# The last eight terms of a head attention's products added on TensorE instead of GpSimd, with a new order of items in a decoder layer

## The chip, the core and the metric
The kernel runs on one core of a Trainium2 chip. The metric is the device time of one execution in microseconds (us). Inside a core TensorE (PE) multiplies matrices into PSUM, VectorE (DVE), ScalarE (ACT) and GpSimd (POOL) work element by element, and SyncE (SP) issues the DMAs. The engines run side by side, each in its own written order, and wait for each other by semaphores.

## The reference
One decoder layer over 2048 tokens of 256 features, fp32, in three parts, each on the layer norm of x and added to x:
```
q, k, v = x@Wq.T, x@Wk.T, x@Wv.T, as 16 heads of 16; q, k rotated (rope); q's heads permuted
scores = einsum('bshd,bstd->bsht', q, k) / 4            # within one token, head against head
attn   = einsum('bsht,bstd->bshd', softmax(scores), v);  x += attn @ Wo.T
q = fake_quant(x@Wxq + b); k, v = fake_quant(cond@Wkv + b)   # 2048 keys, 16 heads of 16
p = fake_quant(softmax(q@k.T));  x += (p@v) @ Wp + b
scores = sigmoid(x@gate.T); two of 8 experts per token; x += shared + routed silu MLP
```
The first part matters here: per token a 16x16 table of scores, each a sum of 16 products over d, and a 16x16 table of outputs, each a sum of 16 products over t.

## The kernel before, in words
The 2048 tokens are 16 tiles of 128 tokens, a token to a partition. A stage ahead of the loop (steps u = 0 to 9) makes the quantised keys and values of all 2048 conditions. Then `body(t)` runs over the tiles, and in it h runs over the 16 heads of the cross attention of tile t. Around this spine lie the other parts, each for another tile: a = t+2 gets layer norm 0, q, k, v, rope and the scores of its head attention; n = t+1 gets the rest of its head attention, layer norm 1 and its quantised queries; m = t-1 gets the end of its cross attention, layer norm 2, gate and shared expert; o = t-2 gets the experts and the store.

The spine of one head: TensorE makes the scores of 128 tokens against 2048 keys in two halves (`scores(h, 0, t)`, `scores(h, 1, t)`, L1459) into two PSUM buffers that take turns. VectorE scales each half into SBUF and takes its minimum (`keep_scores`, L1135), then makes the bias (L1145). ScalarE takes the exponent (`exp_head`, L824). SP issues a DMA transpose of the result (`turn`, L423). TensorE multiplies four transposed heads by the values in 64 products (`times_values(0)`, `(G)`, `(2G)`, `(3G)`, L1489). There are four buffers each of score and prob and six of transposed prob, so turn n waits for the products of head n-6.

Each engine's order is written out by hand: in its `body(t)` a list of items, each with the head h at which it stands, is gone through for every h. On VectorE, TensorE and ScalarE the items stand around the spine's own items. The places that matter, before:
- SP, `body` L435: `turn_routed(t-1)` at h=13, `load_x(t+3)` (L375, waits for one_done) at h=15 ahead of `turn(15, t)`, `store(t-2)` (L403, waits for `add_out` of VectorE) at h=2 behind `turn(2, t)`.
- GpSimd, head attention: `multiply` (L522) makes 4 of the 16 rows at a time into one of four product buffers, 1024 products per partition. `fold_one` (L529) adds terms 8 to 15 to 0 to 7. `fold_8`, `fold_4`, `fold_2` (to L567) add on down to one, over two buffers at a time, into hs (scores) or ho (outputs). `shift_scores` (L478) subtracts the maximum that VectorE found, `norm_ho` (L483) multiplies by the inverse sum.
- VectorE, `body` L1219: `loaded(a)` and bn_stats of x_in (L1075) at h=0 behind `keep_scores(0)`; bn_stats of the projected head attention (L1075, waits for L1424) at h=8; `cross_norm(m)` h=5; `choose(m)` h=10; `largest_score(a)` and `quantise_queries(n)` h=13; `add_out(o)` h=3.
- TensorE, `body` L1563: `ho_turn(n)` and `ho_project(n)` (L1416, L1424) at h=8, the projection right behind `times_values(0, t)`; `times_values(3G, m)` h=5; `times_values(G, t)` h=12; `times_values(2G, t)` h=15.
- ScalarE, `body` L887: `ln_apply(0, a)` behind exp 0, `ln_keep(0, a)` ahead of exp 1, `keep_qkv(0, a)` ahead of exp 2 (L770).

TensorE runs about one head ahead of VectorE, bound by the two buffers:
```
def wait_slot(u):
    if u >= 2:
        kind, n, i = USES[u - 2]
        if kind == "score":
            pe.wait_ge(score_kept, 2 * n + i + 1)
```
The bank `ps_pv` holds the output of times_values in its first 256 columns; `bank` 5, 6 and 7 serve the other products by turns.

## Time and profile before
| | us |
|---|---|
| median of 3 runs | 1065.17 |
| lowest, highest | 1061.33, 1065.57 |
| the profiled execution, its own time | 1068.14 |
| its span in the profile | 1065.7 |
| mean granted clock of TensorE, of 2.4 GHz | 0.838 |

The profiled execution is 3.0 us over the median. In the rows PE is TensorE, PEld its weight loads, DVE VectorE, ACT ScalarE, POOL GpSimd, SPq the DMA queue of SP. L12 is line 12 of the kernel; several products share line 1317, a helper. Loading, keys and values take the time up to 92.5 us, where the first score is read; tile 1 begins at 159 us, tile 14 at 921 us.

### The profile page before, as it was taken

To read this page: it belongs to the slowest core of one execution; us is meant where nothing else is said; L and a number is where in the kernel's file an instruction comes from. 1 tells how busy PE (TensorE), PEld (TensorE's weight loads), DVE (VectorE), ACT (ScalarE), POOL (GpSimd) and SP (SyncE) were. 2 spreads that over 40 slices of the span, in tenths; PEclk is the share of its full clock that TensorE was granted. 3 is DMA by queue.
4 is the path that set the end of the run, shared out by engine and by line. 5 is a ranking of instruction groups with operands and counts; after the bars stand their busy time and mean duration, and the time that the engine had idled before them with its cause. 6 is when DMAs were issued, how large, how long until landed. Compare 5 with 4: busy or idle time off the path is not lost. (4 is left out here: it accounts for less than half of the span.)

```text
span 1065.7 us, 21210 instructions
## 1 busy us (share of the span) xinstructions
PE 722.0 (68%) x7072; PEld 388.6 (36%) x7072; DVE 906.5 (85%) x1841; ACT 737.3 (69%) x989; POOL 746.9 (70%) x728
## 2 busy tenths in 40 slices
PE   6966647666675867675776758576667767675674
PEld 4543323333342524343332425243333324242333
DVE  3887769989888899989898989899888989999851
ACT  2644656868677776868686877778686868878742
POOL 6688987787786778787886868787878868730000
PEclk9975777888896978889897989888878979798965
DMA  6012767979698896979797999979697979999981
GB/s 225 1 40 70 133 119 140 186 115 192 128 176 147 150 173 127 187 114 198 120 194 144 160 168 146 190 121 188 129 179 115 192 150 169 172 167 182 162 161 25
DMA packets 574019, 156.01 MB, mean 146 GB/s; under 512 B 567252, under 2 KB 571863, under 8 KB 573527
## 3 DMA queue, kind: packets, MB, share of 16 engines
q1 hardware_dynamic: 573910, 154.67, 81.5%
q8 instruction: 56, 0.92, 0.3%
q14 instruction: 53, 0.43, 0.1%
HBM read 9.93 MB, written 2.10 MB: 11 GB/s over the span
## 5 line engine op out<-in xcount | busy, mean ns | idle before, releaser
L1135 DVE TENSOR_SCALAR_CACHE_REDUCE score<-ps_score,q_neg 128x1024 f32<-128x1024 f32 x512 | 636.2, 1277 | 17.2 <-PE ps_score L1459 15.9
L824 ACT ACTIVATE prob<-score,exp_bias 128x2048 uint16<-128x2048 f32 x256 | 512.1, 2001 | 61.4 <-DVE exp_bias L1145 58.5
L1459 PE MATMUL ps_score<-keys,queries 128*128 128x512 bf16 x1024 | 368.1, 450 | 255.4 <-DVE score L1135 248.7
L1459 PEld LDWEIGHTS ps_score<-keys,queries 128*128 128x128 bf16 x1024 | 72.2, 103 | 445.7 <-DVE score L1135 415.9
L527 POOL TENSOR_TENSOR product<-hs_exp,v_tok 128x1024 f32<-128x1024 f32 x64 | 149.4, 2347 | 31.0 <-ACT hs_exp L789 30.8
L534 POOL TENSOR_TENSOR product<-product 128x512 f32<-128x512 f32 x128 | 159.5, 1262 | 0.0
L527 POOL TENSOR_TENSOR product<-qk_rot 128x1024 f32<-128x1024 f32 x64 | 150.2, 2349 | 0.3 <-POOL qk_rot L520 0.2
L1489 PE MATMUL ps_pv<-prob_t,values 128*32 128x128 f16 x4096 | 74.2, 229 | 25.1 <-DMA prob_t<-prob 24.8
L545 POOL TENSOR_TENSOR product<-product 128x512 f32<-128x512 f32 x64 | 80.8, 1271 | 5.9 <-POOL product L534 5.9
L1489 PEld LDWEIGHTS ps_pv<-prob_t,values 128*32 128x32 f16 x4096 | 63.2, 101 | 55.2 <-issue 55.2
L466 POOL TENSOR_SCALAR var_eps<-mean_var 128x1 f32<-128x1 f32 x48 | 12.6, 262 | 90.2 <-DVE mean_var L1080 89.2
L884 ACT ACTIVATE early<-ps 128x512 f32<-128x512 f32 x32 | 19.1, 597 | 67.8 <-DVE early L1188 61.6
L768 ACT COPY normed_t<-ps 128x256 f32<-128x256 f32 x48 | 18.0, 376 | 65.1 <-PE ps L1322 65.1
L481 POOL TENSOR_TENSOR hs<-hs,hs_max 128x256 f32<-128x256 f32 x16 | 10.0, 622 | 69.3 <-DVE hs_max L1084 69.3
L1317 PE MATMUL ps<-routed_both,w 128*128 128x128 bf16 x512 | 45.0, 249 | 18.6 <-DMA routed_both<-routed_both 16.9
L877 ACT ACTIVATE routed_both<-normed,routed_gate 128x256 bf16<-128x256 f32 x128 | 55.4, 493 | 1.2 <-DVE routed_gate L1180 1.2
L1145 DVE TENSOR_SCALAR exp_bias<-low 128x1 f32<-128x1 f32 x256 | 52.0, 203 | 2.8
L1317 PEld LDWEIGHTS ps<-routed_both,w 128*128 128x128 bf16 x512 | 39.4, 113 | 35.9 <-DMA routed_both<-routed_both 21.7
L824 ACT ACTIVATION_READ_ACCUMULATOR prob<-score,exp_bias 128x1 f32 x256 | 48.9, 191 | 0.0
L502 POOL COPY sum_wide<-sum_inv 128x128 f32<-128x128 f32 x32 | 8.5, 296 | 52.0 <-DVE sum_inv L1152 52.0
L552 POOL TENSOR_TENSOR product<-product 128x256 f32<-128x256 f32 x64 | 39.7, 629 | 5.9 <-POOL product L545 5.9
L1135 DVE DVE_READ_ACCUMULATOR score<-ps_score,q_neg 128x1 f32 x512 | 42.3, 83 | 0.0
(124 smaller groups left out, 1112.2 us busy)
## 6 DMA issues: line engine op xcount, KB each, us to landing
prob_t<-prob SPq DMA_TRANSPOSE x256, 4.5
prob_t<-in_w SPq DMA_DIRECT2D x3, 1024.0 KB, 4.8
x_in<-in_x SPq DMA_DIRECT2D x16, 128.0 KB, 3.0
score<-in_cond_t SPq DMA_DIRECT2D x4, 512.0 KB, 6.3
out<-x_out SPq DMA_DIRECT2D x16, 128.0 KB, 2.7
w_qkv<-in_w_qkv SPq DMA_DIRECT2D x1, 768.0 KB, 4.4
early<-in_w_kv SPq DMA_DIRECT2D x1, 512.0 KB
w_s<-in_w_s SPq DMA_DIRECT2D x3, 128.0 KB
```

The costliest lines, as they stand in the source:

```text
L527: pool.tensor_tensor(product[:, i % 4], a_, b_, ALU.mult).then_inc(multiplied, 1)
L534: pool.tensor_tensor(terms[:, :, 0:8], terms[:, :, 0:8], terms[:, :, 8:16], ALU.add).then_inc(folded_8, 1)
L545: pool.tensor_tensor(terms[:, :, 0:4], terms[:, :, 0:4], terms[:, :, 4:8], ALU.add).then_inc(folded_4, 1)
L552: pool.tensor_tensor(terms[:, :, 0:2], terms[:, :, 0:2], terms[:, :, 2:4], ALU.add).then_inc(folded_2, 1)
L824: act.activation(prob[:, s, :].bitcast(U16), score[:, s, :], ACT.Exp, bias=exp_bias[:, s:s + 1], scale=-1.0, accum_out=prob_sum[:, t.par, ...
L877: act.activation(routed_tok[:, e, :], normed[:, 2, :], ACT.Copy, scale=routed_gate[:, e:e + 1]).then_inc(routed_made, 1)
L884: act.activation(tanh[:].rearrange("p e q -> p (e q)"), bank[(5, 7)[i]][:, :], ACT.Tanh, scale=0.5).then_inc(hidden_tanhed, 1)
L1135: dve.tensor_scalar(score[:, s, HALF * i:HALF * i + HALF], ps_score[:, score_slot(t.count(H, h), i)].rearrange("p b k -> p (b k)"), q_neg[ ...
L1145: dve.tensor_scalar(exp_bias[:, s:s + 1], low[:, s, 0:1], low[:, s, 1:2], LN255, ALU.min, ALU.add).then_inc(bias_ready, 1)
L1317: mm = pe.matmul(out, lhs[c], rhs[c], start=start and c == 0, stop=stop and c == C - 1)
L1459: mm = pe.matmul(ps_score[:, score_slot(n, i), b, :], queries[:, t.par, h // 2, h % 2, :], keys[:, h // 2, k0:k0 + KEYS], start=True, stop ...
L1489: mm = pe.matmul(out[j], beside_zeros(values, i, h + j), prob_t[:, t.count(H, h + j) % KEPT, i, :], start=(i == 0 and first), stop=(i == T ...
```

## The change
The products of the head attention are folded once on GpSimd, from 16 to 8 terms, and the 8 terms are added by 8 fp32 matmuls with the identity as weights, which accumulate in PSUM (`sum_terms`, four per tile, each over two product buffers, so 128 columns with a step of 16 elements in SBUF). The sums lie in bank 7 for tiles 0 and 1 and in the free half of the bank of `ps_pv` after, and times_values waits for their readers (`wait_pv`). VectorE takes the maximum there, and now also does the shift and the division. hs_exp and ho_n come out as before.

The items of all engines have new places. SP: `store(t-2)` at h=0 ahead of `turn(0, t)`, `load_x(t+3)` at h=13 behind `turn(13, t)`. VectorE: bn_stats of x_in stays at h=0; `add_out(o)` 2, both `expert_hidden(o)` 1, `sum_scores(n)` 1, `cross_sum(m)` 2, `cross_norm(m)` 4, bn_stats(2, m) 5, `norm_ho(n)` 8 and bn_stats(1, n) 10 ahead of keep_scores, `choose(m)` 11, `largest_query(n)` 12, `quantise_queries(n)` 14 and `shift_scores(a)` 15 ahead of keep_scores, `largest_score(a)` 14 behind it. TensorE: `ln_turn(0, a)` 3, `times_values(3G, m)` 4 between the two score halves, `queries_or_keys(a)` and `xo_project(m)` 5, `sum_terms(2, n)` 6 and `(3, n)` 7, `ho_turn(n)` and then `times_values(0, t)` 8, `ho_project(n)` 9, `gate_and_shared(m)` and `times_values(G, t)` 11, `sum_terms(0, a)` 13 and `(1, a)` 14, `q_turn(n)` and `times_values(2G, t)` 15; the sums stand behind scores(h, 1). ScalarE: `ln_apply(0, a)` 2, `ln_keep(0, a)` and `keep_xo(m)` 3, `keep_qkv(a)` 4 and 6, `keep_ho(n)` 7, all ahead of that head's exp, `keep_queries(n)` 14, `head_exp(a)` 15. In tile 0 the items of n come two heads later.

The core of the diff (the re-ordered lists of VectorE, TensorE and ScalarE are the text above):
```diff
         v_tok = sb("v_tok", [P, HD, H])
-        product = sb("product", [P, 4, G, H, HD])
+        product = sb("product", [P, 4, G * H, HD])
+        k_max = sb("k_max", [P, 2 * H])
...
         def own_bank(t):
-            return bank[5 if t.idx < 2 else 7]
+            return bank[5 if t.idx < 3 else 7]
+
+        def sums_of(t):
+
+            return (bank[7] if t.idx < 2 else ps_pv)[:, D:2 * D]
...
             def body(t):
                 for h in range(H):
+                    if (t + -2).exists() and h == 0:
+                        store(t + -2)
                     if (t + -1).exists() and h == 13:
                         turn_routed(t + -1)
-                    if (t + 3).exists() and h == 15:
-                        load_x(t + 3)
                     if t.exists() and by_dma(h):
                         turn(h, t)
-                    if (t + -2).exists() and h == 2:
-                        store(t + -2)
+                    if (t + 3).exists() and h == 13:
+                        load_x(t + 3)
...
-            def shift_scores(t):
-                pool.wait_ge(hs_shift, t.count(2, 1))
-                pool.sem_inc(settled, 1)
-                pool.tensor_tensor(hs[:], hs[:], over(hs_max[:], H), ALU.subtract).then_inc(hs_shift, 1)
-            def norm_ho(t):
-                pool.wait_ge(reduced, t.count(4, 4))
...
-                pool.tensor_tensor(ho_n[:], ho[:], over(hs_inv[:], HD), ALU.mult).then_inc(ho_done, 1)
...
             def multiply(i, t, a_, b_):
-                    pool.wait_ge(reduced, due)
+                    pool.wait_ge(summed, due)
                     pool.sem_inc(settled, 1)
-                pool.tensor_tensor(product[:, i % 4], a_, b_, ALU.mult).then_inc(multiplied, 1)
-            def fold_one(i, t):
+                out = product[:, i % 4].rearrange("p (g h) d -> p g h d", g=G)
+                pool.tensor_tensor(out, a_, b_, ALU.mult).then_inc(multiplied, 1)
+
+            def fold(i, t):
+                terms = product[:, i % 4]
                 pool.wait_ge(multiplied, t.count(8, i + 1))
                 pool.sem_inc(settled, 1)
-                pool.tensor_tensor(terms[:, :, 0:8], terms[:, :, 0:8], terms[:, :, 8:16], ALU.add
...
-            def fold_8(i, t):
-                terms = both(i)
-                pool.wait_ge(folded_8, t.count(8, 2 * i + 2))
-                pool.sem_inc(settled, 1)
...
-            def fold_4(i, t):
...
-            def fold_2(i, t):
...
+                pool.tensor_tensor(terms[:, :, 0:HD // 2], terms[:, :, 0:HD // 2], terms[:, :, HD // 2:HD],
+                                   ALU.add
+                    ).then_inc(folded, 1)
...
             def body(t):
                 a, n, m = t + 2, t + 1, t + -1
                 if n.exists():
-                    value_products(2, n)
-                if m.exists():
-                    spread_sums(m)
+                    value_products(0, n)
+                    fold(4, n)
+                    value_products(1, n)
+                    fold(5, n)
                 if a.exists() and not t.starts():
                     ln_scale(0, a)
                 if n.exists():
+                    value_products(2, n)
+                    fold(6, n)
+                if m.exists():
+                    spread_sums(m)
+                if n.exists():
                     value_products(3, n)
-                    fold_one(6, n)
-                    fold_one(7, n)
-                    fold_8(3, n)
-                    fold_4(3, n)
-                    fold_2(3, n)
+                    fold(7, n)
                 if a.exists():
                     rope(a)
-                if n.exists():
-                    norm_ho(n)
-                if a.exists():
                     score_products(0, a)
+                    fold(0, a)
                 if m.exists():
                     ln_scale(2, m)
                 if a.exists():
                     score_products(1, a)
-                    fold_one(0, a)
+                    score_products(2, a)
+                    fold(1, a)
+                    score_products(3, a)
                 if n.exists():
                     ln_scale(1, n)
                 if a.exists():
-                    score_products(2, a)
-                    fold_one(1, a)
-                    score_products(3, a)
-                    fold_one(2, a)
-                    fold_one(3, a)
-                    fold_8(0, a)
-                    fold_8(1, a)
-                    fold_4(0, a)
-                    fold_4(1, a)
-                    fold_2(0, a)
-                    fold_2(1, a)
-                    shift_scores(a)
-                    value_products(0, a)
-                    value_products(1, a)
-                    fold_one(4, a)
-                    fold_one(5, a)
-                    fold_8(2, a)
-                    fold_4(2, a)
-                    fold_2(2, a)
...
             def all_scores(t):
-                score_products(0, t)
...
-                fold_2(1, t)
+                for j in range(0, G, 2):
+                    score_products(j, t)
+                    score_products(j + 1, t)
+                    fold(j, t)
+                    fold(j + 1, t)
+
+            def half_values(j, t):
+                value_products(j, t)
+                value_products(j + 1, t)
+                fold(G + j, t)
+                fold(G + j + 1, t)
...
             def largest_score(t):
-                dve.wait_ge(reduced, t.count(4, 2))
-                dve.tensor_reduce(hs_max[:], hs[:], AX.X, ALU.max).then_inc(hs_shift, 1)
+                dve.wait_ge(summed, t.count(4, 2))
+                dve.tensor_reduce(hs_max[:], heads(sums_of(t)), AX.X, ALU.max).then_inc(hs_shift, 1)
+
+            def shift_scores(t):
+                dve.wait_ge(hs_shift, t.count(2, 1))
+                if (due := t.due(1)) is not None:
+                    dve.wait_ge(hs_exped, due)
+                dve.tensor_tensor(hs[:], heads(sums_of(t)), over(hs_max[:], H), ALU.subtract).then_inc(hs_shift, 1)
+
+            def norm_ho(t):
+                dve.wait_ge(summed, t.count(4, 4))
+                dve.wait_ge(hs_summed, t.count(2, 2))
+                if (due := t.due(1)) is not None:
+                    dve.wait_ge(ho_turned, due)
+                dve.tensor_tensor(ho_n[:], heads(sums_of(t)), over(hs_inv[:], HD), ALU.mult).then_inc(ho_done, 1)
...
@@ -1287,18 +1213,20 @@
                     loaded(second)
                     ln_gather(0, x_in[:, 1, :], second)
                     ln_combine(0, second)
-                if u == 4:
                     largest_score(first)
+                    shift_scores(first)
                 if u == 5:
                     value_maxima(0)
                 if u == 6:
+                    cast_experts(0)
                     sum_scores(first)
                     invert_sums(first)
-                    cast_experts(0)
-                if u == 8:
+                    norm_ho(first)
+                if u == 7:
                     dve.wait_ge(ho_projected, 1)
                     ln_gather(1, one_bank(first)[:, 0:D], first)
                     ln_combine(1, first)
...
@@ -1306,6 +1234,8 @@
             cast_experts(1)
             keep_first_values(0)
             keep_first_values(1)
+            largest_score(second)
+            shift_scores(second)
...
             def ho_turn(t):
                 pe.wait_ge(ho_done, t.count(1, 1))
-                if t.starts():
-                    pe.wait_ge(qkv_kept, 4)
+                if t.idx < 2:
+                    pe.wait_ge(qkv_kept, t.count(2, 4))
...
@@ -1477,10 +1407,9 @@
                         pe.wait_ge(prob_turned[n % KEPT], 16 * count_dma(n + 1, n % KEPT))
                 if (made := count_pe(t.count(H, h + G))) > 0:
                     pe.wait_ge(turn_kept, made)
-                if h == 0:
-
-                    if (due := t.due(1)) is not None:
-                        pe.wait_ge(xo_kept, due)
+                wait_pv()
+                if h == 3 * G:
+                    read["xo"] = t.idx + 1
...
+            read = {"shift": 0, "ho": 0, "xo": 0}
+
+            def wait_pv():
+
+                if read["shift"] > 0:
+                    pe.wait_ge(hs_shift, 2 * read["shift"])
+                if read["ho"] > 0:
+                    pe.wait_ge(ho_done, read["ho"])
+                if read["xo"] > 0:
+                    pe.wait_ge(xo_kept, read["xo"])
+
+            def sum_terms(i, t):
+
+                pe.wait_ge(folded, t.count(8, 2 * i + 2))
+                if t.idx < 2:
+                    if i == 2:
+                        pe.wait_ge(hs_shift, t.count(2, 2))
+                    if t.idx == 1 and i == 0:
+                        pe.wait_ge(ho_done, 1)
+                else:
+                    wait_pv()
+                out = sums_of(t)[:, P * (i % 2):P * (i % 2) + P]
+                for d in range(HD // 2):
+                    mm = pe.matmul(out, ident[:], product[:, 2 * (i % 2):2 * (i % 2) + 2, :, d], start=d == 0,
+                                   stop=d == HD // 2 - 1)
+                mm.then_inc(summed, 1)
+                if t.idx > 1 and i % 2 == 1:
+                    read[("shift", "ho")[i // 2]] = t.idx + 1
...
@@ -1649,10 +1614,18 @@
                 if u == 9:
                     ln_turn(1, first)
                     xq(first)
+                if u == 4:
+                    sum_terms(1, first)
+                if u == 6:
+                    sum_terms(2, first)
+                if u == 7:
+                    sum_terms(3, first)
                 keys_and_values(u)
+                if u == 3:
+                    sum_terms(0, first)
+                if u == 4:
+                    ln_turn(0, second)
                 if u == 5:
-                    ln_turn(0, second)
-                if u == 6:
                     queries_or_keys(0, second)
                     queries_or_keys(1, second)
                     own_values(0, second)
@@ -1662,6 +1635,8 @@
             q_turn(first)
             turn_values(2)
             turn_values(3)
+            sum_terms(0, second)
+            sum_terms(1, second)
```

## Rows read from the trace of the kernel before

**Rows 1.** The page, part 1: busy time, share of the span, instructions of each engine
```profile
PE 722.0 (68%) x7072; PEld 388.6 (36%) x7072; DVE 906.5 (85%) x1841; ACT 737.3 (69%) x989; POOL 746.9 (70%) x728
```

**Rows 2.** Busy time by stretch: stretch, length, engines, TensorE clock share, DMA share, GB/s
```profile
686.10:744.40 58.30, 39.18 (x428) 21.07 (x426) 53.23 (x112) 43.98 (x60) 46.18 (x46) 0.88 0.94 160
921.10:973.00 51.90, 34.87 (x402) 17.97 (x402) 50.25 (x109) 42.54 (x57) 19.12 (x22) 0.93 0.99 175
```

**Rows 3.** Waits of VectorE, 158.9 to 921.2 us: total us, times, longest
```profile
DVE stats L1075 <- DMA x_in<-in_x: 37.4, 13, 3.8
DVE stats L1075 <- PE ps L1424: 25.7, 13, 3.8
```

**Rows 4.** Timeline of VectorE: start us, us, instruction, idle before and releaser
```profile
159.00 0.41 DVE L1088 TENSOR_REDUCE hs_sum<-hs_exp 128x16 f32<-128x256 f32 x1
...
744.36 0.41 DVE L1088 TENSOR_REDUCE hs_sum<-hs_exp 128x16 f32<-128x256 f32 x1
...
750.56 0.43 DVE L1075 BATCH_NORM_STATS2 stats<-x_in 128x6 f32<-128x256 f32 x1 [3.07 <-DMA x_in<-in_x]
...
778.72 0.43 DVE L1075 BATCH_NORM_STATS2 stats<-ps 128x6 f32<-128x256 f32 x1 [3.25 <-PE ps L1424]
...
921.13 0.41 DVE L1088 TENSOR_REDUCE hs_sum<-hs_exp 128x16 f32<-128x256 f32 x1
```

**Rows 5.** Timeline of SP's queue; the last row is 10 transposes issued without a gap
```profile
747.39 0.93 SPq L380 DMA_DIRECT2D x_in<-in_x  x1
...
755.13 1.44 SPq L423 DMA_TRANSPOSE prob_t<-prob  x1
...
766.57 1.86 SPq L423 DMA_TRANSPOSE prob_t<-prob  x1
...
769.71 1.90 SPq L423 DMA_TRANSPOSE prob_t<-prob  x1
...
994.11 27.09 SPq L423 DMA_TRANSPOSE prob_t<-prob  x10
```

**Rows 6.** Timeline of TensorE's products
```profile
663.47 0.69 PE L1317 MATMUL ps<-normed_t,w_s 128*128 128x128 f32 x4
...
770.49 0.59 PE L1459 MATMUL ps_score<-keys,queries 128*128 128x512 bf16 x2
...
774.50 1.78 PE L1489 MATMUL ps_pv<-prob_t,values 128*32 128x128 f16 x64 [1.01 <-DMA prob_t<-prob]
```

**Rows 7.** Groups by line, GpSimd: busy us, mean ns | idle before
```profile
L545 POOL TENSOR_TENSOR product<-product 128x512 f32<-128x512 f32 x64 | 80.8, 1271 | 5.9 <-POOL product L534 5.9
L552 POOL TENSOR_TENSOR product<-product 128x256 f32<-128x256 f32 x64 | 39.7, 629 | 5.9 <-POOL product L545 5.9
L567 POOL TENSOR_TENSOR ho<-product 128x128 f32<-128x128 f32 x32 | 13.0, 406 | 7.0 <-POOL product L552 7.0
L491 POOL TENSOR_TENSOR ho_n<-ho,hs_inv 128x256 f32<-128x256 f32 x16 | 10.0, 624 | 0.6 <-POOL ho L567 0.6
```

**Rows 8.** Groups by line, VectorE: an operation of 128x256 with an operand in PSUM
```profile
L1160 DVE TENSOR_TENSOR xo_t<-ps,xo_raw 128x256 f32<-128x256 f32 x16 | 6.7, 420 | 3.1 <-PE ps L1500 3.1
```

**Rows 9.** Groups by line: TensorE's fp32 products of 128 columns, ScalarE's copies from PSUM
```profile
L1317 PE MATMUL ps<-normed_t,w_s 128*128 128x128 f32 x128 | 21.5, 294 | 0.0
L768 ACT COPY normed_t<-ps 128x256 f32<-128x256 f32 x48 | 18.0, 376 | 65.1 <-PE ps L1322 65.1
L780 ACT COPY v_tok<-ps 128x256 f32<-128x256 f32 x16 | 9.6, 598 | 2.1 <-POOL product L527 0.9 <-PE ps L1405 0.6
```

**Rows 10.** Timeline of TensorE's products in the last tile's tail
```profile
1046.33 2.05 PE L1317 MATMUL ps<-normed_t,w_s 128*128 128x128 f32 x8
```

**Rows 11.** Waits of VectorE, 93 to 158.9 us
```profile
DVE hs_max L1084 <- POOL hs L567: 10.2, 2, 7.3
DVE score L1135 <- PE ps_score L1459: 9.3, 5, 3.8
```

**Rows 12.** Busy time by stretch, in the stage ahead of the loop (columns as in Rows 2)
```profile
28.00:66.00 38.00, 35.67 (x194) 21.68 (x194) 33.09 (x55) 22.83 (x34) 29.45 (x26) 1.00 0.09 29
```

367 lines of the change are left out of this document (155 added, 212 removed).

## Prediction
> **What bounds the kernel now.** I read the busy shares first: VectorE is busy 85% of the span, GpSimd 70%, ScalarE 69%, TensorE 68% [rows 1]. Then two stretches of one tile each: in a tile of 58.3 us VectorE is busy 53.2 us, GpSimd 46.2, ScalarE 44.0, TensorE 39.2, and the DMA share is 0.94 [rows 2]. So VectorE sets the pace, and what can still be won is its idle time. The list of its waits from 158.9 to 921.2 us names it [rows 3]: 37.4 us in 13 waits for x_in and 25.7 us in 13 waits for TensorE's projection of the head attention (line 1424), with 2.3 us of others 65.4 in all. From hs_sum of tile 1 at 159.00 to hs_sum of tile 14 at 921.13 13 tiles take 762.1 us, 58.6 each, and the timeline shows one wait of each sort per tile, in the one that starts at 744.4 of 3.07 and 3.25 us [rows 4]. Without them a tile would take 53.6 us.
>
> Why they are there: load_x(t+3) stands before turn(15, t) in SP's queue and comes out only after turn(14, t). It is issued at 747.39 and lands 3 us later, while bn_stats stands ready behind head 0 [rows 4, 5]. The second wait ends with the projection: TensorE stands 1.01 us for the transposed head 3 (turn 3 was issued at 769.71, 25 us into the tile, behind the store), then does 64 products in 1.78 us and right behind them the projection, in one burst with two score buffers before it [rows 4 to 6].
>
> **The change, part by part.**
>
> 1. *GpSimd loses* the folds of 8, 4 and 2 terms, the shift and the division: 80.8 + 39.7 + 13.0 for ho and 12.2 for hs in a like group + 10.0 for the division and as much for the shift = 165.7 us, 10.4 per tile [rows 7]. The fold from 16 to 8 stays. In the steady state I cost this at nothing: GpSimd has 12 us of slack per tile. It counts early on, where GpSimd is late: VectorE waits 10.2 us for hs in tile 0 [rows 11].
>
> 2. *VectorE gains* two operations of 128x256 from PSUM. The nearest row is the 128x256 tensor_tensor from PSUM, 420 ns [rows 8]: 0.84 us per tile, and nothing covers it, since VectorE is the bound. Bounds 0.7 to 1.0. For 13 tiles +10.9 us.
>
> 3. *TensorE gains* four sums of 8 fp32 identity products per tile, each a 128x128 product. By w_s, one such product is two records, so a sum is 16 records. At the full clock 4 records take 0.69 us [rows 6], of which about 0.15 is the latency of the last, as a score pair of 0.59 us shows against 0.43 for 2 x 512 columns at 2.4 GHz: some 0.13 to 0.14 each. At the low clock 8 take 2.05, or 0.26 each [rows 10]; the mean over the kernel is 21.5/128 = 0.168 [rows 9]. A sum is thus 2.1 us at 2.4 GHz, 4.1 at 1.2, 2.7 in the mean, and TensorE goes from 39.2 to about 50 us per tile, under VectorE's 54.4. What counts is where the bursts lie, because scores have two buffers only. Between scores(h,1) and scores(h+1,0) VectorE has two score operations of 1.2 us and the bias to do, 2.6 us, of which the two score products take 0.9: a burst up to 1.6 is hidden. At h=6 a sum of 2.1 to 2.7 shows 0.5 to 1.1. At h=7 the division (0.42) follows, slack 1.9: 0.2 to 0.8. At h=13 the 2.2 us of quantise_queries come next, slack 4. At h=14 they come before largest_score needs the sum, slack 3.5; at 4.1 us that one shows 0.6. I take 1.2 us per tile, nearest to the full clock rows, because a score pair ahead of h=7 takes 0.59 us already, the full clock's time [rows 6], and the idle time of TensorE behind the x_in wait goes. Bounds 0 and 5 (all sums at 4.1). For 13 tiles +15.6 us.
>
>    What no row shows is a moving operand read with a step of 16 fp32. The nearest row is on another engine: ScalarE's copy into v_tok writes 256 elements with such a step in 598 ns, the plain copy of 256 takes 376 [rows 9]. So from below it costs nothing; from above it takes 598/376 = 1.6 of the time, 3.4 us a sum at full clock. I take nothing, since the fp32 product here is paced by its two records with their own weight loads, not by elements alone, and keep the other end as a rival. The Trainium skill (SBUF — State Buffer, section Door 1) says SBUF has 16-byte lines and that each access to a new line pays, so a stride is free only to 4 fp32; by that rule this operand pays on every element and the time would be that of the first rival. The v_tok row agrees with it; on TensorE no row of this trace tells.
>
>    The sums lie in the bank of ps_pv from tile 2 on, so times_values and the sums wait for the last reader of that bank. times_values(0) at h=8 waits for ho_done, times_values(2G) at h=15 for the shift that VectorE now does ahead of head 15. Behind it in TensorE's queue are scores(9,0) and the next tile's scores. Both readers run about 0.6 and 1.0 us after VectorE frees the second buffer, TensorE needs 0.45 of that for scores: under 0.6 us, inside the slack. GpSimd's products wait for summed: the score products 0 for the sum at h=6, when it still does rope. Nothing.
>
> 4. *x_in* moves from h=15 before turn(15) to h=13 behind turn(13): one head, 3.4 us, earlier, against a wait of about 3.0. It goes, with 0.4 us to spare. bn_stats stays at h=0 and needs the load at 2.5 us into the tile. Queued ahead of it are turn_routed and turn 13 as before. Gain 37.4 us.
>
> 5. *Projection.* norm_ho is now on VectorE at h=8, ho_project on TensorE at h=9, behind the 64 products instead of in one burst with them, and bn_stats(1) on VectorE at h=10, two heads later than before. The wait of 25.7 us goes. Late next would be the products, if turn 3 is late.
>
> 6. *The store* moves from h=2 behind turn(2) to h=0 ahead of turn(0), and waits for add_out, now VectorE's at h=2. So SP stands until about 12 us into the tile (heads 0 to 2 of VectorE with both expert_hidden: 3.1 + 5.8 + 3.0). Queued behind it are turns 0, 1 and 2. Turn 0 goes at 13, instead of 10.8; but turn 2, which now waits for times_values(3G) at h=4, goes at 18.4 instead of 22.2, and turn 3 at 21 instead of 25.3, landing at 25.6 [rows 5]. TensorE wants it at about 27. exp_head(4) needs turn 0 at 17.5 and ScalarE sees it at 18: 0.5 us there, hidden by four score buffers. But a backlog clears at 2.7 us a transpose (10 in 27.09 us) [rows 5]: 17 x 2.7 + x_in and store 1.8 + 7 us of standing = 54.7 us. That is no more than VectorE's period, but no less. I cost it at nothing.
>
> 7. *The other moves* (layer norm chain on ScalarE one to three heads later) remove ScalarE's waits before exp 1 and 2; it is no bound. POOL's queue: ln_scale(0), behind fold(5), now waits for the bn_aggr at h=2, behind it are value products 2 and 3. They end at 18 us into the tile, and their sums stand at h=6 and 7, 20 us and later: free.
>
> 8. *Before tile 1.* 20.6 us of VectorE's gaps lie between 93 and 159: 10.2 for hs, 9.3 for scores [rows 11]. I count 12 of them as gone. In the staged part before, TensorE is busy 35.7 of 38 us, VectorE 33.1 [rows 12], and sums of tile 0 are put there: two are bare, some 4 us, the other two lie beside value_maxima and cast_experts; VectorE's own additions partly fill its gaps. Tile 0's loop waits for tile 1's scores now, but that wait only moves ahead of it. Net 12 - 3 = 9, bounds 0 and 14. In the tail (144.6 us from tile 14 on) the transposes are the bound [rows 2] and the sum there is nil, +-2.
>
> **Sum.** 9 + 65.4 - 10.9 - 15.6 = 47.9 us less, against the profiled execution's own 1068.1 us (span 1065.7 and 2.4 around it): 1020.2. The median of the runs shown, 1065.2, is 3.0 lower: **1017 us**.
>
> **Rivals.**
> - *The bursts show* (chance 0.20): the step of 16 doubles the moving time, or the clock stays low. With 3.4 us a sum, h=6 shows 1.8 and h=7 1.5, 3.3 us per tile instead of 1.2: +28, 1045 us. For it the v_tok row, against it the slow fp32 pace.
> - *SP's queue sets the pace* (0.12): the store blocks the turns, SP's 54.7 us become 57 with a later add_out, x_in arrives late and VectorE waits 2 us more per tile: 1043 us. For it the DMA share of 0.94; against it that turn 2 was no earlier before.
> - *Slower* (0.12): one mechanism, the price of a sum. Past 4 us of a sum every slack is used up (1.6 + 1.9 + 4 + 3.5 = 11), and 4 x S - 11 us per tile show. The gains without a stall are 63.5 us, 4.9 per tile, so it decides at S = 4.0, 0.25 us a record. At 5 us, 2.4 times the full clock's price, it is 9 us per tile: 1017 + 13 x 7.8 = 1118 us. The low clock row lies just at that point [rows 10].
> - *Nothing shows* (0.06): no stall at all, 1002 us. That the change does not do what it says I can exclude: the folds are gone from GpSimd's code.
>
> **Numbers.** The forecast case has 0.50, from 1003 to 1030. The range of 1003 to 1054 adds most of the two middle cases and leaves the slower case and a bit at either end. About 0.5%, 5 us, is what a measurement of this kernel tells from no change. Faster: 0.50 + 0.06 + most of 0.32 = 0.80; within 0.5% 0.07; slower 0.13.
>
> **What would show it.** Right: bn_stats of x_in and of line 1424 without a wait; 64 sums of 16 records, each 2.1 to 2.7 us; a period of about 55.6 us; VectorE's share near 90%; GpSimd's near 56%. Wrong: VectorE's score operation waiting for scores behind the sums by over 2 us, sums over 3 us, or SP's turns late with ScalarE waiting for prob_t in every tile.

## The result, and the profile after

The changed kernel takes **1090.2 us** (median of 4 runs, 1089.5 to 1090.7); the kernel before, beside it, 1064.5. The ratio is 1.025, 95% interval 1.022 to 1.027: slower, where 1017 us were forecast and the range ended at 1054. The profiled execution took 1089.5 us (span 1087.7).

First the page, part 1, to be held against [rows 1]:

```profile
PE 885.9 (81%) x8096; PEld 592.5 (54%) x8096; DVE 902.7 (83%) x1873; ACT 740.4 (68%) x989; POOL 586.7 (54%) x504
```

GpSimd lost 160 us (165.7 forecast). TensorE gained 164: the sums take 233, and its other work fell from 722 to 653 with a mean granted clock that rose from 0.838 to 0.924. VectorE's share did not rise to 90%, it fell to 83%. The groups by line give the price of what was added, and the timeline of TensorE shows the four sums of one tile (start, length, count of records):

```profile
L1446 PE MATMUL ps_pv<-product,ident 128*128 128x128 f32 x896 | 204.3, 394 | 0.0
```
```profile
666.51 3.65 PE L1446 MATMUL ps_pv<-product,ident 128*128 128x128 f32 x16
671.29 3.65 PE L1446 MATMUL ps_pv<-product,ident 128*128 128x128 f32 x16
691.81 3.65 PE L1446 MATMUL ps_pv<-product,ident 128*128 128x128 f32 x16
696.15 3.65 PE L1446 MATMUL ps_pv<-product,ident 128*128 128x128 f32 x16
```

A sum takes 3.65 us, not 2.1, and it is not the clock: that length stands at the full clock, and 58 of the 64 sums have it. It is 204.3/896 = 0.228 us a record, against 21.5/128 = 0.168 of w_s [rows 9]. VectorE's waits over the whole span (total us, times, longest) answer to [rows 3], which cover only the loop:

```profile
DVE score L1059 <- PE ps_score L1389: 29.5, 26, 2.8
DVE ho_n L1008 <- PE ps_pv L1446: 22.0, 14, 1.6
...
DVE hs_max L995 <- PE ps_pv L1446: 17.9, 14, 1.6
DVE early L1109 <- ACT early L793: 14.8, 13, 1.3
DVE hs_max L995 <- PE ps L1446: 13.5, 2, 8.6
DVE stats L986 <- PE ps L1472: 11.8, 14, 2.3
...
DVE stats L986 <- PE ps L1354: 1.0, 1, 1.0
```

The two waits of before are gone: the one for the projection (now line 1354) is 1.0 us instead of 25.7, and the one for x_in no longer stands among the large ones. In their place are waits for line 1446, the sums. (The wait for line 1472, the projection of the cross attention, is new too but not one of theirs: it stays at 0.7 to 0.8 us per tile with one product per sum.) The timeline of VectorE shows the waits behind the sums in one tile (heads 0, 6, 7 and 14; the last number is the idle time before):

```profile
648.41 0.69 DVE L1109 SCALAR_TENSOR_TENSOR early<-early,ps 128x512 f32<-128x512 f32 x1 [1.15 <-ACT early L793]
...
670.63 1.28 DVE L1059 TENSOR_SCALAR_CACHE_REDUCE score<-ps_score,q_neg 128x1024 f32<-128x1024 f32 x1 [1.44 <-PE ps_score L1389]
674.98 0.42 DVE L1008 TENSOR_TENSOR ho_n<-ps_pv,hs_inv 128x256 f32<-128x256 f32 x1 [1.60 <-PE ps_pv L1446]
...
699.84 0.43 DVE L995 TENSOR_REDUCE hs_max<-ps_pv 128x16 f32<-128x256 f32 x1 [1.19 <-PE ps_pv L1446]
```

Each of the last three stands right behind a sum. The first is a detour of the same cause. The timeline of ScalarE:

```profile
641.29 2.04 ACT L715 COPY queries<-ps 64x1024 bf16<-64x1024 bf16 x2 [3.06 <-PE ps L1368]
...
647.80 0.58 ACT L793 ACTIVATE early<-ps 128x512 f32<-128x512 f32 x1
```

ScalarE stands 3.06 us for q_turn, which is behind sum 1 on TensorE, and reaches the tanh at head 0 that much later. Ahead of the loop the sums stand in bursts of two. VectorE waits at 44.89 and again right ahead of the first score:

```profile
44.89 0.42 DVE L995 TENSOR_REDUCE hs_max<-ps 128x16 f32<-128x256 f32 x1 [4.91 <-PE ps L1446]
...
111.29 0.42 DVE L995 TENSOR_REDUCE hs_max<-ps 128x16 f32<-128x256 f32 x1 [8.62 <-PE ps L1446]
112.09 1.27 DVE L1059 TENSOR_SCALAR_CACHE_REDUCE score<-ps_score,q_neg 128x1024 f32<-128x1024 f32 x1
...
169.65 1.28 DVE L1059 TENSOR_SCALAR_CACHE_REDUCE score<-ps_score,q_neg 128x1024 f32<-128x1024 f32 x1 [0.46 <-PE ps_score L1389]
...
941.71 1.28 DVE L1059 TENSOR_SCALAR_CACHE_REDUCE score<-ps_score,q_neg 128x1024 f32<-128x1024 f32 x1
```

These score operations open tiles 0, 1 and 14. With the same marks in every kernel the span divides as follows (us; the time of one of tiles 1 to 13 is called the period below; "term outside" and "one product" are experiments):

| | before | changed | term outside | one product |
|---|---|---|---|---|
| start of tile 0 | 92.6 | 112.1 | 102.9 | 98.1 |
| tile 0 | 67.4 | 57.6 | 53.7 | 53.5 |
| tiles 1 to 13, each | 58.6 | 59.4 | 54.75 | 54.2 |
| tile 14 | 50.9 | 56.0 | 53.8 | 53.1 |
| tile 15 and tail | 93.3 | 90.0 | 90.5 | 90.9 |

Before to changed: 19.5 later at the start, 9.9 won in tile 0, 10.6 lost in the 13 tiles, 5.0 in tile 14, 3.3 won at the end.

### The profile page after: what moved, and what is told of

It reads as the page before. It is cut to its first block, busy times and chain, and to the rows that moved or that the text cites. A ratio compares the mean times of both kernels' runs of the same rounds, so it can differ in the third digit from the quotient of the medians.

```text
span 1087.7 us, 22982 instructions
## 1 busy us (share of the span) xinstructions
PE 885.9 (81%) x8096; PEld 592.5 (54%) x8096; DVE 902.7 (83%) x1873; ACT 740.4 (68%) x989; POOL 586.7 (54%) x504
## 4 chain that ended last, share of the span: by engine, by line
PE 47%; DVE 22%; ACT 12%; issue 12%; SPq 3%; DMA 2%; POOL 1%; ACTq 0%; DVEq 0%; POOLq 0%
PE ps_pv L1446 18%; DVE score L1059 14%; PE ps_score L1389 9%; ACT prob L733 9%; PE ps L1247 6%; PE ps L1446 3%; SPq L424 2%; PE ps_score L1247 2%; DVE early L1109 2%; PE ps_pv L1418 2%; DVE gate L1093 1%; PE ps L1335 1%; PE ps L1252 1%; DMA routed_both<-routed_both 1%; PE ps L1472 1%
## 5 line engine op out<-in xcount | busy, mean ns | idle before, releaser
L1389 PE MATMUL ps_score<-keys,queries 128*128 128x512 bf16 x1024 | 318.5, 406 | 118.1 <-DVE score L1059 108.2
L1389 PEld LDWEIGHTS ps_score<-keys,queries 128*128 128x128 bf16 x1024 | 80.6, 101 | 253.1 <-DVE score L1059 198.0
L1446 PE MATMUL ps_pv<-product,ident 128*128 128x128 f32 x896 | 204.3, 394 | 0.0
L1446 PEld LDWEIGHTS ps_pv<-product,ident 128*128 128x128 f32 x896 | 184.2, 211 | 16.8 <-issue 0.3
L521 POOL TENSOR_TENSOR product<-product 128x512 f32<-128x512 f32 x128 | 160.8, 1263 | 13.2 <-POOL product L514 13.2
L1247 PE MATMUL ps<-routed_both,w 128*128 128x128 bf16 x512 | 41.3, 237 | 40.6 <-DVE early L1112 28.9
L467 POOL TENSOR_SCALAR var_eps<-mean_var 128x1 f32<-128x1 f32 x48 | 10.6, 222 | 99.3 <-DVE mean_var L991 97.6
L1247 PEld LDWEIGHTS ps<-routed_both,w 128*128 128x128 bf16 x512 | 35.7, 107 | 50.5 <-issue 31.9
L715 ACT COPY queries<-ps 64x1024 bf16<-64x1024 bf16 x32 | 32.2, 1007 | 39.9 <-PE ps L1368 39.6
L1109 DVE SCALAR_TENSOR_TENSOR early<-early,ps 128x512 f32<-128x512 f32 x32 | 21.9, 685 | 25.3 <-ACT early L793 14.8
L488 POOL COPY sum_wide<-sum_inv 128x128 f32<-128x128 f32 x32 | 8.4, 291 | 58.6 <-DVE sum_inv L1076 58.6
L1252 PE MATMUL ps<-ident,normed 128*128 128x128 f32 x96 | 21.1, 303 | 20.3 <-ACT normed L669 20.1
```

The source lines that it names most:

```text
L521: pool.tensor_tensor(terms[:, :, 0:HD // 2], terms[:, :, 0:HD // 2], terms[:, :, HD // 2:HD], ALU.add).then_inc(folded, 1)
L715: act.copy(queries[rows, t.par, :, j, :], bank_bf[5][rows, :].rearrange("p (a q) -> p a q", q=P)).then_inc(q_kept, 1)
L1109: dve.scalar_tensor_tensor(out=th, in0=th, scalar=1.0, in1=first_, op0=ALU.add, op1=ALU.mult).then_inc(chain, 1)
L1247: mm = pe.matmul(out, lhs[c], rhs[c], start=start and c == 0, stop=stop and c == C - 1)
L1389: mm = pe.matmul(ps_score[:, score_slot(n, i), b, :], queries[:, t.par, h // 2, h % 2, :], keys[:, h // 2, k0:k0 + KEYS], start=True, stop ...
L1446: mm = pe.matmul(out, ident[:], product[:, 2 * (i % 2):2 * (i % 2) + 2, :, d], start=d == 0, stop=d == HD // 2 - 1)
```

## The experiments

Theory A is that the step of 16 fp32 in the moving operand doubles the time of a sum and the longer bursts cost the rest; B, that fp32 itself has this price; C, that the new order of items costs the time. Every median stands beside runs of the kernel before of the same call (1064.3 to 1065.3 us).

### Reading 128 contiguous fp32

```diff
-mm = pe.matmul(out, ident[:], product[:, 2*(i%2):2*(i%2)+2, :, d], ...
+mm = pe.matmul(out, ident[:], product[:, 2*(i%2), 0:HD//2, :], ...
```

> The moving operand of the 8 identity products of a sum is 128 contiguous fp32 instead of 128 at a step of 16; nothing else changes (the sums add other terms than they should). Theory A, the step doubles the moving time: a record falls from 0.23 us to 0.13 to 0.15, a sum from 3.65 to 2.1 to 2.4 us at full clock, VectorE's stalls behind the sums at heads 6, 7 and 13 (1.4, 1.6, 1.2 to 1.4 us per tile) nearly go, the period falls from 59.4 us by about 4, and the time to about 1030 us. Theory B, the price is that of fp32 itself, two records with a weight load each: a sum stays at 3.65 us and the time at 1090. Theory C, the new order costs the time and not the sums: sums shorten and the time stays above 1075.

**1012.4 us**, ratio to before 0.951 (0.946 to 0.955). One access pattern, nothing else, is worth 78 us. The group of the sums:

```profile
L1446 PE MATMUL ps_pv<-product,ident 128*128 128x128 f32 x896 | 109.2, 275 | 0.9 <-POOL product L521 0.9
```

0.122 us a record instead of 0.228. B and C are out. It came out 18 us better than A expected: the period fell by 5.05 us, not by 4, which is 14 us over the 13 tiles, and the start and tiles 0 and 14 gained 14.7 us, where about 8 of the expected 60 us are left for them.

### One product per sum

```diff
-for d in range(HD // 2):
+for d in range(1):
```

> One identity product per sum instead of eight, so seven of the eight terms are left out; order, waits, GpSimd and VectorE as in the changed kernel. Theory A: a sum takes 0.5 us, no stall behind it is left, 14 tiles x 4.3 us and some 10 us of the stage before tile 0 come back: 1015 to 1020 us, and a period near 54.8. Theory C, the new order costs the time: it stays above 1075. If it lands between 1030 and 1060, sums and order have a part each.

**1003.7 us** (0.943, 0.939 to 0.948), 11 us below the least that A expected; the period is 54.2. So the eight products, read contiguously, cost 9 us in all; at the step of 16 they cost 86.5.

### The term outside: the same result with contiguous reads

```diff
-product = sb("product", [P, 4, G * H, HD])
+product = sb("product", [P, 4, HD, G * H])
 # GpSimd's product
-out = product[:, i % 4].rearrange("p (g h) d -> p g h d", g=G)
+out = product[:, i % 4].rearrange("p d (g h) -> p g h d", g=G)
 # fold
-terms[:, :, 0:HD//2], terms[:, :, 0:HD//2], terms[:, :, HD//2:HD]
+terms[:, 0:HD//2], terms[:, 0:HD//2], terms[:, HD//2:HD]
 # sum
-product[:, 2*(i%2):2*(i%2)+2, :, d]
+product[:, 2*(i%2):2*(i%2)+2, d, :]
```

> The product buffer is laid out with the term d outermost, so that each identity product reads two runs of 64 contiguous fp32 and the fold adds contiguous halves; GpSimd's product writes at a step of 64 fp32 instead. The whole result is computed. Theory A: sums as in the dense read, 2.1 to 2.4 us. If GpSimd writes at that step as fast as before, the time is that of the dense read, about 1030 us; if its product slows by half (8 products per tile, some 2.1 us each, +8 us per tile), GpSimd goes to about 45 us per tile, still under the period, and the time is 1035 to 1050; if it doubles, GpSimd is the bound and the time is above 1090.

**1012.4 us** (0.951, 0.948 to 0.954), as the dense read. GpSimd pays nothing for writing at a step of 64 fp32 (groups by line of this kernel, then of the changed one):

```profile
L514 POOL TENSOR_TENSOR product<-qk_rot 128x1024 f32<-128x1024 f32 x64 | 151.4, 2380 | 7.0 <-PE ps_pv L1446 6.4 <-POOL qk_rot L506 0.5
```
```profile
L514 POOL TENSOR_TENSOR product<-qk_rot 128x1024 f32<-128x1024 f32 x64 | 150.8, 2367 | 29.2 <-PE ps_pv L1446 28.6 <-POOL qk_rot L506 0.5 <-issue 0.2
```

This is the change with its flaw removed; it takes 5% less time than the kernel before and 7% less than the changed one.

### Two folds on GpSimd

```diff
 # behind the fold from 16 to 8 terms, a fold from 8 to 4
+pool.wait_ge(folded_8, t.count(8, i + 1))
+pool.tensor_tensor(terms[:, :, 0:4], terms[:, :, 0:4], terms[:, :, 4:8], ALU.add).then_inc(folded, 1)
 # sum
-for d in range(HD // 2):
+for d in range(HD // 4):
```

> GpSimd folds once more, from 8 terms to 4, and TensorE adds 4 by identity products. The whole result is computed. Theory A: a sum takes 1.8 us, half of the stalls behind sums and more go, GpSimd gains 8 folds of 256 elements, some 6 us per tile, under its slack: a period near 55.5 and about 1030 us. Theory of GpSimd's lateness: the second fold delays the score products at heads 8 to 14 and the sums at 13 and 14 wait for it: above 1060. Theory C: above 1075.

**1084.3 us** (1.016, 1.011 to 1.021). A sum is down to 1.90 us, and still the period is 59.2: the theory of GpSimd's lateness, though by another way than expected. GpSimd has 5.8 us more per tile, and in the timelines of GpSimd, ScalarE and TensorE one wait follows from the other:

```profile
747.19 0.23 POOL L468 TENSOR_SCALAR var_eps<-mean_var 128x1 f32<-128x1 f32 x1
```
```profile
748.67 0.60 ACT L675 ACTIVATE normed<-x_one,shift,rstd 128x256 f32<-128x256 f32 x1 [2.86 <-POOL shift L476]
```
```profile
749.33 0.44 PE L1258 MATMUL ps<-ident,normed 128*128 128x128 f32 x2 [3.12 <-ACT normed L675]
```

### Two folds, ln_scale(1) ahead of score products 3

```diff
-score_products(3, a)
 ln_scale(1, n)
+score_products(3, a)
```

> The kernel with two folds on GpSimd (1084 us; its reads keep the step of 16) with ln_scale(1, next tile) ahead of score products 3 instead of behind them in GpSimd's queue, 2.4 us earlier; the statistics it needs are there 3.7 us before. The whole result is computed. Theory E, the second fold costs time because GpSimd reaches ln_scale(1) late, ScalarE's normed with it, and TensorE stands 3.1 us per tile ahead of the scores of head 12: TensorE's wait falls from 3.1 to about 0.7 us, the period from 59.2 to about 57, the time to about 1055. Rival, the sums at heads 6, 7, 13 and 14 come late by the longer folds themselves: 1080 to 1085 as before the move.

**1057.5 us** (0.992, 0.989 to 0.995) and a period of 57.3, as theory E had it. That is 1.8 us of the 4.4 that the second fold cost per tile; the other 2.6 were not followed. TensorE's wait for normed, first in the kernel with two folds, then here:

```profile
PE ps L1258 <- ACT normed L675: 73.2, 40, 8.6
```
```profile
PE ps L1258 <- ACT normed L675: 38.3, 35, 8.3
```

### The places of the first stage

```diff
 # GpSimd
-ln_scale(1, first)
 all_scores(second)
+ln_scale(1, first)
 # TensorE
 ho_turn(first)
+sum_terms(0, second)
+sum_terms(1, second)
 ho_project(first)
...
 turn_values(3)
-sum_terms(0, second)
-sum_terms(1, second)
```

> The kernel with the term outside (1012.4 us), with two moves ahead of the loop: on GpSimd all score products of tile 1 stand ahead of ln_scale(1, tile 0), for which GpSimd idles some 20 us; on TensorE the sums 0 and 1 of tile 1 stand between ho_turn and ho_project of tile 0, where TensorE waits 4.4 us for ScalarE, instead of right ahead of the first scores, where VectorE waits 4.9 us for them. The whole result is computed. Theory D, the first stage lost by the place of the sums and GpSimd's queue: the first score operation comes 4 to 8 us sooner and the time is 1004 to 1009. Rival, TensorE's own work bounds that stage whatever the order: 1011 to 1014.

**1012.9 us** (0.951, 0.949 to 0.952): half right. The first score comes 4.0 us sooner (98.93), but tiles 0 and 14 take 3.8 us longer and the time is unchanged. Why these give it back was not followed further.

### The store at head 2

```diff
-if (t + -2).exists() and h == 0: store(t + -2)
 turn(h, t)
+if (t + -2).exists() and h == 2: store(t + -2)
```

> The kernel with the term outside (1012.4 us), with the store back behind turn 2 of head 2, as it was before. The whole result is computed. The prediction's step, the store's place costs nothing: 1010 to 1015 us. Rival, SP standing 7 to 9 us per tile for x_out is what is left to win: 1000 to 1007. Rival, the place at head 0 helps because turn 2 no longer waits for the store: slower, 1018 or more.

**1010.7 us** (0.950, 0.946 to 0.953), not told apart from 1012.4 by these runs: the place of the store costs nothing.

### The load alone in the kernel before, put back in the new one, and earlier still

```diff
-if (t + 3).exists() and h == 15: load_x(t + 3)   # ahead of turn
 turn(h, t)
+if (t + 3).exists() and h == 13: load_x(t + 3)
```

> The kernel before with one move: load_x(t+3) at head 13 behind turn 13 instead of at head 15 ahead of turn 15. The whole result is computed. The prediction's step 4 counts 37.4 us for it: if the wait goes and nothing takes its place, 1027 us, with a period near 55.7. Rival, another wait takes its place (the projection, the head attention's terms on GpSimd, SP's turns late by the load ahead of turn 14): 1045 to 1065, and the period stays above 57.

**1032.7 us** (0.969, 0.967 to 0.971), period 55.9. This one move is worth 32.6 us, 5 less than part 4 of the prediction counts. VectorE's waits in it: the one for x_in has shrunk, the one for the projection stands as it was.

```profile
DVE stats L1075 <- PE ps L1424: 25.7, 15, 3.3
...
DVE stats L1075 <- DMA x_in<-in_x: 4.9, 4, 3.0
```

> The kernel with the term outside (1012.4 us) with load_x back at head 15 ahead of turn 15, as it was before. The whole result is computed. If the wait for x_in is worth in this order what it was in the old one (32.6 us by moving it alone, 2.5 per tile): 1040 to 1050. Rival, in the new order SP is further ahead at head 15 or the wait is hidden by VectorE's longer tile: 1012 to 1030.

**1037.6 us** (0.974, 0.971 to 0.976), 2 us under the expected range: the load moved back costs 25 us in the new order, with the same wait:

```profile
DVE stats L986 <- DMA x_in<-in_x: 40.6, 14, 4.3
```

That is 7 less than in the old order; waits of VectorE for score products, 20.3 us in the kernel with the term outside, are 15.6 here.

One head earlier still, on the kernel with the store at head 2:

```diff
-if (t + 3).exists() and h == 13: load_x(t + 3)
+if (t + 3).exists() and h == 12: load_x(t + 3)
```

> The kernel with the term outside, with the store behind turn 2 (1010.7 us) and load_x one head earlier again, at head 12 behind turn 12. The whole result is computed. If what is left of the wait for x_in (10 us in 10 waits) is worth its length: 1002 to 1006. Rival, the load and the transposes share one queue whose transfers fill the period (DMA share 1.02 in a tile), so what x_in wins turn 13 loses, or VectorE's own 53.1 us of work per tile is the bound: 1008 to 1013.

The time is **1018.4 us** (0.958, 0.953 to 0.963). The waits for x_in in the loop go, those for score products rise to 31.6 us, from 19.1 with the store at head 2, and the period is 55.05. It is slower than both expectations, by 5 us at least; nothing was won there.

### The price by step

```diff
+step = 2 << i
+spread = product[:, 2*(i%2):2*(i%2)+2].rearrange("p r g d -> p (r g d)")[:, 0:P * step]
-product[:, 2*(i%2):2*(i%2)+2, :, d]
+spread.rearrange("p (n s) -> p n s", s=step)[:, :, d % step]
```

> The price of a record of an fp32 identity product by the step of its moving operand, other terms than the kernel needs: sum 0 reads at a step of 2 fp32, sum 1 of 4, sum 2 of 8, sum 3 of 16. Theory A in the form of the lines: steps 2 and 4 cost what the contiguous read costs, 1.95 us a sum, step 8 and 16 3.65. Rival, each element pays in proportion: 2 is already dearer. Rival, only a step over 8 pays.

Timeline of TensorE, in this order sums 0, 1, 2 and 3, at steps of 2, 4, 8 and 16 fp32:

```profile
624.19 1.98 PE L1448 MATMUL ps_pv<-product,ident 128*128 128x128 f32 x16
627.05 3.79 PE L1448 MATMUL ps_pv<-product,ident 128*128 128x128 f32 x16
656.98 3.88 PE L1448 MATMUL ps_pv<-product,ident 128*128 128x128 f32 x16
661.99 3.65 PE L1448 MATMUL ps_pv<-product,ident 128*128 128x128 f32 x16
```

The edge lies between 2 and 4, one place sooner than expected, and beyond it the price is flat. The kernel took 1075.3 us (1.009, 1.006 to 1.012).

### Longer sums with contiguous reads; long sums at one place

```diff
-for d in range(HD // 2):        # term outside, 8 products
+for d in range(HD):             # "twice": 16; "half more": range(12)
-product[:, 2*(i%2):2*(i%2)+2, d, :]
+product[:, 2*(i%2):2*(i%2)+2, d // 2, :]
```

> The kernel with the term outside, each identity product done twice in its sum, so that every term counts double: 32 records of 0.12 us instead of 16, with contiguous reads. Theory A, only the length of the burst counts: a sum takes 3.8 to 3.9 us, the period goes from 54.8 back to 59.4 or a little above, and the time to 1088 to 1097. Rival, the step costs beyond its own burst (the reads disturb what other engines read from the same memory): well below that, 1040 to 1075.

**1110.3 us** (1.042, 1.040 to 1.045), period 60.9. Contiguous reads that last as long cost as much and more, so no cost of the step beyond its own burst shows. It is 13 us over the expected; nine of the sums, all at head 13, took 1.15 to 1.43 us longer, as the first row here, where TensorE's granted clock is 0.50 (1.2 GHz) at its start (645.7 to 647.0 us), 1.00 in the second's:

```profile
645.74 4.94 PE L1446 MATMUL ps_pv<-product,ident 128*128 128x128 f32 x32
651.38 3.73 PE L1446 MATMUL ps_pv<-product,ident 128*128 128x128 f32 x32
```

> The kernel with the term outside with 12 identity products per sum instead of 8, reading contiguously (four terms count double): 24 records, a sum of some 2.85 us, between the 1.95 of that kernel and the 3.65 of the changed one. The prediction's slacks of 1.6 and 1.9 us at heads 6 and 7 and more than 3 at 13 and 14: 1.25 + 0.95 = 2.2 us per tile over the 54.2 of the kernel with one product, a period of 56.4 and about 1036 us. Rival, one straight line from 1.95 us (54.75) to 3.65 (59.4): 57.2 and some 1050. Rival, a knee: what is under 3 us stays hidden: below 55.3 and under 1022.

**1060.4 us** (0.996, 0.994 to 0.998), period 57.9. That is over both the forecast's slacks (56.4) and the straight line (57.2). Timelines of VectorE and of TensorE:

```profile
627.71 0.69 DVE L1109 SCALAR_TENSOR_TENSOR early<-early,ps 128x512 f32<-128x512 f32 x1 [1.09 <-ACT early L793]
...
649.12 1.28 DVE L1059 TENSOR_SCALAR_CACHE_REDUCE score<-ps_score,q_neg 128x1024 f32<-128x1024 f32 x1 [0.63 <-PE ps_score L1389]
652.66 0.42 DVE L1008 TENSOR_TENSOR ho_n<-ps_pv,hs_inv 128x256 f32<-128x256 f32 x1 [0.79 <-PE ps_pv L1446]
...
677.71 0.42 DVE L995 TENSOR_REDUCE hs_max<-ps_pv 128x16 f32<-128x256 f32 x1 [0.61 <-PE ps_pv L1446]
```
```profile
645.81 2.84 PE L1446 MATMUL ps_pv<-product,ident 128*128 128x128 f32 x24
649.78 2.84 PE L1446 MATMUL ps_pv<-product,ident 128*128 128x128 f32 x24
670.62 3.51 PE L1446 MATMUL ps_pv<-product,ident 128*128 128x128 f32 x24
674.83 2.84 PE L1446 MATMUL ps_pv<-product,ident 128*128 128x128 f32 x24
```

The third row of TensorE, sum 0 at head 13, takes 3.51 us instead of 2.84, with a granted clock of 0.50 (1.2 GHz) from 669.0 to 672.0 us and 1.00 after; in 11 tiles this sum takes 3.4 us or more. In the changed kernel no sum in the loop is so lengthened. So the two kernels with longer contiguous sums carry a cost of the clock beside that of the length, and the 0.7 us over the straight line was not separated from it.

```diff
+terms = (product[:, 2*(i%2):2*(i%2)+2, :, d] if i > 1   # sums 2, 3: the step of 16
+         else product[:, 2*i, 0:HD//2, :])              # sums 0, 1: contiguous
-mm = pe.matmul(out, ident[:], product[:, 2*(i%2):2*(i%2)+2, :, d], ...
+mm = pe.matmul(out, ident[:], terms, ...
```

> The changed kernel with sums 2 and 3 (heads 6 and 7) at the step of 16 and sums 0 and 1 (heads 13 and 14) reading 128 contiguous fp32, so that these two add other terms: which place pays. By the waits seen in the changed kernel (1.44 and 1.60 us per tile at heads 6 and 7, 1.2 to 1.4 at 14 and 1.15 for ScalarE's early at head 0): a period of 56.8 to 57.5 with the wait for early still short, and 1045 to 1055 us. Rival, the two places share one slack and half of the length costs less than half: below 56 and under 1040.

**1063.6 us** (0.998, 0.997 to 1.000), period 57.9. The waits at heads 6 and 7 are 1.44 and 1.60 us to the digit, whatever the sums at 13 and 14 do. The wait for hs_max is gone; the one for early is 0.56 in the tile looked at. The period is 0.4 over what was expected, and the time 9 us over the expected range; the 54.75 of the term outside plus 1.44 and 1.60 gives 57.8, so these two places make up the period here.

## Why the prediction was wrong

**The step that failed is in part 3: "What no row shows is a moving operand read with a step of 16 fp32 ... I take nothing".** Its reason, that the fp32 product is paced by its records' own weight loads, is refuted by the dense read: the weight loads are the same there, and a record goes from 0.228 to 0.122 us. The other end of the bound, 1.6 times and 3.4 us, was nearly right (3.65, 1.87 times the 1.95 of the dense read), and it came from the one row with such a step [rows 9]. The Trainium skill (SBUF — State Buffer, section Door 1) was cited against the change, and the direction of its rule holds on TensorE too. The passage counts a stride of up to 4 fp32 as free and also asks for at least two hits on each 16-byte line; by the measurement a step of 2 fp32, two hits on a line, is free (1.98 us) and one of 4, one hit, already pays in full (3.79), so the trace agrees with the second statement and not with the first. With contiguous reads the forecast stands: 1012.4 against 1017.

**The second error is what a burst shows.** The rival with the right price gave 1045, not 1090. At heads 6 and 7 the waits grow one for one with the sum, over three lengths: 3.65 - 1.44 = 2.84 - 0.63 = 3.73 - 1.52 = 2.21 us hidden at head 6 (the third length is that of the doubled products), and 3.65 - 1.60 = 2.84 - 0.79 = 2.05 at head 7. The forecast had 1.6 and 1.9, so the two buffers hide a little more. It was wrong elsewhere: at 13 and 14 together 7.30 - 1.19 = 6.1 us are hidden, not 4 + 3.5, and it is no fixed length there (3.51 + 2.84 - 0.61 = 5.7 with half more products); ScalarE's detour by q_turn adds 1.15 us, which no step had; and the stage ahead of the loop, costed at "two sums bare, some 4 us", starts 14.0 us later than with one product per sum (and 5.5 of the 19.5 us lost there stay even with one). From one product to eight at the step of 16 the spans differ by 87.8 us: 67.7 in the 13 tiles (the rival 43), 14.0 ahead of tile 0, 4.1 and 2.8 in tiles 0 and 14, -0.9 after. The slower rival named the right mechanism, with its break-even at a sum of 4.0 us; the half-more kernel, 2.84 us (3.5 at head 13) and 0.4% under before, puts it near 3.

Against the forecast the span is 70 us longer: 49.5 in tiles 1 to 13 (38.9 to be won, 10.6 lost), 18.7 ahead of tile 1 (9 to be won, 9.7 lost) and 1.7 from tile 14 on.

Point by point:
- *Part 1, GpSimd's relief is worth nothing*: wrong in the new order; in the old one it was not tried. With 5.8 us per tile given back (two folds) the period rises by 4.4 over that of the term outside, though its sums (1.90 us) are not longer; moving ln_scale(1) ahead of one product gives 1.8 of them back; GpSimd's 12 us of slack are no slack for ln_scale(1), which stands behind its products.
- *Part 2*: right, 0.42 us for each of the two operations.
- *Part 4, x_in, 37.4 us*: right but a little high; the move alone gives 32.6 and its undoing costs 25.
- *Part 5, the projection's wait goes*: right, 25.7 became 1.0; what it is worth by itself was not tried.
- *Part 6, the store costs nothing*: right, 1.7 us inside the uncertainty. SP's 54.7 us did not become the bound: with one product per sum the period is 54.2, under it, so that estimate was too high.
- *Part 8, 9 us won before tile 1*: 9.7 lost in the changed kernel, 3.3 won with the term outside. That the sums compete there with keys and values, in a stage where TensorE is busy 35.7 of 38 us [rows 12], was read and priced too low: from 28 to 66 us TensorE is now busy 37.35 of 38 us.
- *From tile 14 on nil, +-2*: right, 5.0 lost in tile 14 and 3.3 won after it.
- *Nothing shows, 1002 us*: one product per sum gives 1003.7, so the base of the sum came out right, but partly by luck. In the 13 tiles VectorE is busy 668.8 us there, against 687.1 before and 10.9 more in the forecast; and it waits 27.2 us that the forecast had not: 10.3 for line 1472, 9.8 for scores, 4.9 for x_in, 2.2 for early. A missed gain of 29 us (most of it described below) hid the missed waits.

## What to carry to other kernels

Before work goes to TensorE, look at the innermost step of the moving operand as well as at its type and size: here a layout that costs the producer nothing decides between 5% faster and 2.5% slower. When an added operation has no row, and one row elsewhere in the trace shows its awkward property to be dear, that row is the estimate and not only the far end. A burst between two uses of a pair of buffers was hidden up to a fixed length (2.21 and 2.05 us at heads 6 and 7) and showed one for one beyond it. What is queued behind it serves other engines too; follow those before adding up slacks.

## What the hardware showed that was not expected

**The step.** An fp32 moving operand costs the same at steps of 1 and 2 (1.95 and 1.98 us a sum) and 1.9 to 2.0 times as much at 4, 8 and 16 (3.79, 3.88 and 3.65). GpSimd's products written at a step of 64 take 2.380 us, at a step of 1 2.367: no cost to speak of.

**VectorE behind GpSimd.** VectorE has 15.7 us less busy time with the term outside (890.8) than before (906.5), though it got two operations more. Groups by line of the kernel before, and below those of the kernel with the term outside:

```profile
L1169 DVE SCALAR_TENSOR_TENSOR gate<-gate,b_expert 128x8 f32<-128x8 f32 x16 | 29.9, 1866 | 0.5
L1180 DVE SCALAR_TENSOR_TENSOR routed_gate<-gate 128x8 f32<-128x8 f32 x16 | 8.1, 507 | 0.6
L1167 DVE TENSOR_SCALAR gate<-gate_tanh 128x8 f32<-128x8 f32 x16 | 7.2, 450 | 4.8 <-ACT gate_tanh L863 4.8
```
```profile
L1104 DVE SCALAR_TENSOR_TENSOR routed_gate<-gate 128x8 f32<-128x8 f32 x16 | 14.2, 886 | 0.6
...
L1093 DVE SCALAR_TENSOR_TENSOR gate<-gate,b_expert 128x8 f32<-128x8 f32 x16 | 2.7, 168 | 0.5
L1091 DVE TENSOR_SCALAR gate<-gate_tanh 128x8 f32<-128x8 f32 x16 | 2.7, 168 | 4.8 <-ACT gate_tanh L772 4.8
```

Three operations of 8 elements take 45.2 us before and 19.6 here, 1.6 us less per tile. An operation that else takes 0.17 us can last as long as a GpSimd operation beside it: the one of line 1169 runs from 724.91 for 2.25 us, and GpSimd's product ends at 727.14 (timelines of before):

```profile
724.91 2.25 DVE L1169 SCALAR_TENSOR_TENSOR gate<-gate,b_expert 128x8 f32<-128x8 f32 x1
```
```profile
724.81 2.33 POOL L527 TENSOR_TENSOR product<-qk_rot 128x1024 f32<-128x1024 f32 x1
```

The Trainium skill (SBUF — State Buffer, section SBUF: two separate sides) has a rule for this: the two engines share a pair of ports, and a VectorE operation with two SBUF operands waits for the whole of a GpSimd operation that reads SBUF. The times fit it; no run here takes that meeting away by itself. It is a gain that the forecast had not counted, and with the term outside it covers the 0.84 us of part 2 and more. But less work on GpSimd is not enough to explain it: the changed kernel has the same GpSimd operations as the one with the term outside, and the three take 25.7 us there (VectorE busy 902.7 in all); with two folds GpSimd is busy 92 us longer and they take 20.2. The times point to which of them falls on a long GpSimd operation; that was not isolated:

```profile
L1093 DVE SCALAR_TENSOR_TENSOR gate<-gate,b_expert 128x8 f32<-128x8 f32 x16 | 15.8, 988 | 0.6
```

This row is the operation of line 1169 in the changed kernel, at 0.988 us in the mean, against 1.866 before and 0.168 with the term outside.
